# Gated cross attention and a mixture of experts: x also loaded transposed, keys centred by a second product, gamma in a second copy of the keys

## The reference, cut to what matters

```python
x = x + tanh(g_xattn[0]) * xattn(layernorm(x), ctx, W_k, b_k, gamma, beta)
x = x + tanh(g_ffn[0]) * moe(layernorm(x), ...)

def xattn(p, k_v, W_k, b_k, gamma, beta):
    kv = k_v @ W_k.T + b_k                        # keys, 256 x 64 per batch
    out = einsum('bij,bjd->bid', p, kv)           # query
    sim = einsum('bid,bjd->bij', out, kv) * 256 ** -0.5
    mu, var = mean(sim, -1), var(sim, -1)
    sim = (sim - mu) * rsqrt(var + 1e-6) * gamma + beta
    return softmax(sim, -1)
```

## Time and profile before

| | |
|---|---|
| runs, us | 206.59, 206.69, 211.18 (median 206.69) |
| span of the profiled execution | 204.2 us, 2910 instructions |
| PE busy | 186.4 us (91%) |
| DVE busy | 173.8 us (85%) |
| ACT busy | 83.5 us (41%) |
| POOL busy | 95.0 us (46%) |
| chain that ended last | PE 48%, DVE 36%, DMA 5%, issue 5%, ACT 3% |
| transfers | 18.06 MB |

### The profile page before, as it was taken

The page is one execution under the profiler, slowest core; times in us unless marked ns, Lnnn a source line. Parts: engine busy times, 40 slices in busy tenths (PEclk is TensorE's granted clock), DMA queues, the critical chain, the costliest instruction groups (busy, mean ns, idle before and its releaser), DMA issues.

```text
span 204.2 us, 2910 instructions
## 1 busy us (share of the span) xinstructions
PE 186.4 (91%) x809; PEld 142.1 (70%) x809; DVE 173.8 (85%) x332; ACT 83.5 (41%) x164; POOL 95.0 (46%) x101
## 2 busy tenths in 40 slices
PE   7899799859999979897999798999999999999992
PEld 5555578638687657575778566788888888888871
DVE  0859968999899889999889999998988989889853
ACT  2448527323349633333438314233333433434210
POOL 2252352723741746464444534446665466654500
PEclk9999979999999999999999999999999999999998
DMA  6977000003853525250211000321121122221403
GB/s 152 319 226 220 21 0 0 0 0 76 290 159 128 164 98 167 88 171 12 92 62 51 0 3 0 100 62 51 62 78 65 51 51 78 75 53 51 154 0 106
DMA packets 10264, 18.06 MB, mean 88 GB/s; under 512 B 1741, under 2 KB 3789, under 8 KB 10254
## 3 DMA queue, kind: packets, MB, share of 16 engines
q1 hardware_dynamic: 9760, 17.37, 26.7%
q10 hardware_dynamic: 494, 0.57, 1.3%
HBM read 16.82 MB, written 1.11 MB: 88 GB/s over the span
## 4 chain that ended last, share of the span: by engine, by line
PE 48%; DVE 36%; DMA 5%; issue 5%; ACT 3%; DVEq 1%; POOL 0%; SPq 0%; ACTq 0%
PE bank L794 26%; PE bank L838 14%; DVE act_hi L563 5%; DVE act_f L544 4%; DVE act_lo L566 4%; DVE weighted L536 4%; DMA xs<-x_in 3%; DVE logit L495 2%; DVE stats L458 2%; DMA w_row<-weight_rows 2%; PE bank L741 1%; PE bank L724 1%; PE bank L871 1%; DVE ln L470 1%; DVE x L514 1%
## 5 line engine op out<-in xcount | busy, mean ns | idle before, releaser
L279 POOL TENSOR_TENSOR w_lo<-w_raw,w_hi 128x256 fp32r<-128x256 f32 (+1 forms) x72 | 83.6, 1178 | 69.2 <-ACT w_hi L322 68.3
L322 ACT CAST w_hi<-w_raw 128x256 fp32r<-128x256 f32 (+2 forms) x72 | 36.7, 514 | 61.0 <-PE bank L838 36.1
L794 PE MATMUL bank<-hT_hi,w_hi 128*128 128x512 f32 x142 | 56.5, 398 | 0.0
L794 PE MATMUL bank<-hT_lo,w_hi 128*128 128x512 f32 x142 | 56.3, 396 | 0.0
L794 PE MATMUL bank<-hT_hi,w_lo 128*128 128x512 f32 x142 | 44.6, 395 | 0.0
L566 DVE TENSOR_TENSOR act_lo<-act_f,act_hi 128x512 fp32r<-128x512 f32 (+1 forms) x37 | 39.6, 1073 | 1.2
L380 ACT ACTIVATE silu_g<-bank 128x512 f32<-128x512 f32 x36 | 21.6, 600 | 31.9 <-PE bank L794 31.8
L794 PEld LDWEIGHTS bank<-hT_hi,w_lo 128*128 128x128 f32 x142 | 26.7, 188 | 6.4
L794 PEld LDWEIGHTS bank<-hT_hi,w_hi 128*128 128x128 f32 x142 | 26.7, 188 | 6.4
L838 PE MATMUL bank<-act_hi,w_hi 128*128 128x512 f32 (+1 forms) x74 | 23.6, 400 | 8.0 <-DVE act_hi L563 7.9
L794 PEld LDWEIGHTS bank<-hT_lo,w_hi 128*128 128x128 f32 x142 | 26.7, 188 | 6.1
(11 more groups left out here) (103 smaller groups left out, 143.8 us busy)
## 6 DMA issues: line engine op xcount, KB each, us to landing
w_row<-weight_rows SPq DMA_DIRECT2D x31, 256.0 KB, 3.2
w_raw<-w_in SPq DMA_DIRECT2D x18, 384.0 KB, 3.7
xs<-x_in SPq DMA_DIRECT2D x4, 256.0 KB, 5.9
out<-x SPq DMA_DIRECT2D x4, 256.0 KB, 2.8
cw<-ctxw_in ACTq DMA_DIRECT2D x1, 276.2 KB
vec<-vecs_in ACTq DMA_DIRECT2D x1, 265.0 KB, 5.6
weight_rows<-w_blk SPq DMA_DIRECT2D x4, 16.0 KB
gw<-route_in ACTq DMA_DIRECT2D x1, 16.0 KB, 6.2
```

Source lines behind the costliest of these rows:

```text
L279: nc.gpsimd.tensor_tensor(w_lo[:, par, cols], w_raw[:, bass.ds(n, 1), cols].rearrange("p o c -> p (o c)"), w_hi[:, par, cols].bitcast(F32) ...
L322: nc.scalar.copy(w_hi[:, par, cols], w_raw[:, bass.ds(n, 1), cols].rearrange("p o c -> p (o c)"))\
L794: last = nc.tensor.matmul(dst, w[:, par, w0 + c * P:w0 + (c + 1) * P], m, start=i == 0, stop=i == len(parts) - 1, skip_group_check=True)
```

## The change

x is loaded a second time, transposed on the host, and the query is formed from it as it is, without normalisation. The keys are centred: the sum of a batch's context columns, times W_k over -256, is added in the accumulator by a second product, for both layouts. The first layernorm's variance enters as an epsilon per row that is added to the similarity's variance. For batches 0 and 1 a copy of the keys times gamma gives a second similarity, and the logits are read straight from PSUM; for batches 2 and 3 DVE multiplies by gamma into `scaled`. The transposes of x, their copies, the first layer's roots and its normalisations are gone. `cw` is loaded in two parts with batch 0's context first. The orders of all engines are rewritten, and `x_stats(2)` and `x_stats(3)` stand behind `hidden_low(1)`.

```diff
-        lnT_ps = [bank[0], bank[1], bank[6], bank[7]]
-        qT_ps = [bank[2], bank[3], bank[6], bank[7]]
-        sim_ps = [bank[0], bank[1], bank[6], bank[7]]
+        kv_ps = bank[4]
+        kvT_ps = [bank[5], bank[3], bank[5], bank[3]]
+        qT_ps = [bank[2], bank[2], bank[2], bank[5]]
+        sim_ps, scaled_ps = [bank[0], bank[1], bank[6], bank[7]], [bank[6], bank[7]]
...
+            def load_x(b):
                 sp.dma_start(xs[:, 2 * b:2 * b + 2, :], x_v[:, 2 * b:2 * b + 2, :]).then_inc(x_in[b], 16)
+
+            def load_xT(b):
+                sp.dma_start(xT[:, b, :, :].rearrange("p c t -> p (c t)"), xt[b]).then_inc(xT_in[b], 16)
+
+            load_xT(0)
+            load_x(0)
+            load_xT(1)
+            load_x(1)
+            load_slice(0, 0)
+            load_xT(2)
+            load_xT(3)
+            load_slice(1, 1)
+            load_x(2)
+            load_x(3)
             ahead = 8
-            for n in range(ahead):
-                if n >= 2:
-                    sp.wait_ge(w_in[n % 2], 16 * (n // 2))
+            for n in range(2, ahead):
+                sp.wait_ge(w_in[n % 2], 16 * (n // 2))
...
-            for b in range(B):
-                root(0, b)
             pool.wait_ge(gwhi_ready, 1)
             nc.gpsimd.tensor_tensor(gw_parts[:, :, E:2 * E], gw[:], gw_parts[:, :, 0:E].bitcast(F32), ALU.subtract)\
               .then_inc(gwlo_ready, 1)
             low_gu(0, 0, 0)
             root(1, 0)
             root(1, 1)
-            pool.wait_ge(scaled_ready, 1)
-            nc.gpsimd.tensor_tensor(x1[:, 3, :], prob[:, 3, :], xs[:, 3, :], ALU.add).then_inc(x1_ready[1], 1)
             root(2, 0)
             root(2, 1)
             pool.wait_ge(hid_ready[1], 2)
...
+            first = CD + S
+            act.dma_start(cw[:, 0:first], ctxw[:, 0:first]).then_inc(ctx0_in, 16)
+            act.dma_start(cw[:, first:CD + B * S], ctxw[:, first:CD + B * S]).then_inc(ctx_in, 16)
...
             kv_copy(0)
             kvT_copy(0)
+            q_copy(0)
+            kv_copy(1)
             kvT_copy(1)
             act.wait_ge(vec_in, 16)
             nc.scalar.activation(gates[:], vec[:, V_GATES:V_GATES + 2], ACT.Tanh).then_inc(gates_ready, 1)
-            nc.scalar.activation(gamma_scaled[:], gamma, ACT.Copy, scale=SIM_SCALE).then_inc(gamma_ready, 1)
+            q_copy(1)
             act.wait_ge(gw_in, 16)
             nc.scalar.copy(gw_parts[:, :, 0:E], gw[:]).then_inc(gwhi_ready, 1)
-            ln_copy(0)
-            ln_copy(1)
-            q_copy(0)
             high_gu(0, 0, 0, 16, False)
-            kv_copy(1)
-            q_copy(1)
+            kv_copy(2)
             kvT_copy(2)
-            act.wait_ge(shift_ready, 1)
-            for t in range(HALF, NT):
-                nc.scalar.activation(ln[:, t, :], xs[:, t, :], ACT.Identity, scale=rstd[:, 0, t:t + 1],
-                                     bias=shift[:, t - HALF:t - HALF + 1]).then_inc(ln_ready[t // 2], 1)
+            kv_copy(3)
+            kvT_copy(3)
             softmax_exp(0)
-            kvT_copy(3)
-            ln_copy(2)
-            ln_copy(3)
-            softmax_exp(1)
             q_copy(2)
             q_copy(3)
-            act.wait_ge(scale_ready[1], 1)
-
-            nc.scalar.activation(prob[:, 3, :], prob[:, 3, :], ACT.Copy, scale=attn_scale[:, 3:4])\
-              .then_inc(scaled_ready, 1)
+            softmax_exp(1)
             high_d(0, 0, 0, False)
             high_gu(1, 1, 1, 16, False)
...
+            def context_sum(b):
+                nc.vector.tensor_reduce(ctx_sum[:, b:b + 1], cw[:, CD + b * S:CD + (b + 1) * S], AX.X, ALU.add)\
+                  .then_inc(ctx_sum_ready, 1)
+
+            def keys_gamma(b):
+
+                dve.wait_ge(kvT_ready, b + 1)
+                nc.vector.tensor_tensor(kvT_gamma[:, b * S:(b + 1) * S], kvT[:, b * S:(b + 1) * S],
+                                        gamma[0:CD, :], ALU.mult).then_inc(kvT_gamma_ready, 1)
 
...
             def x_stats(b):
                 dve.wait_ge(x_in[b], 16)
-                mean_var(0, b, lambda t: xs[:, t, :], 1.0, LN_EPS)
-
-            def sim_of(b, t):
-                return sim_ps[b][:, (t % 2) * S:(t % 2 + 1) * S]
+                ts = mean_var(0, b, lambda t: xs[:, t, :])
+                link(nc.vector.tensor_scalar(row_eps[:, ts], meanvar[:, 0, ts, 1], ROW_EPS, ROW_EPS * LN_EPS,
+                                             ALU.mult, ALU.add))
...
             def sim_stats(b):
                 dve.wait_ge(sim_done[b], 1)
-                mean_var(1, b, lambda t: sim_of(b, t), SIM_SCALE ** 2, SIM_EPS)
-
-            def sim_centre(b):
+                ts = mean_var(1, b, lambda t: columns(sim_ps[b], t))
+                nc.vector.tensor_tensor(var_eps[:, 1, ts], meanvar[:, 1, ts, 1], row_eps[:, ts], ALU.add)\
+                  .then_inc(var_ready, 1)
+
+            def sim_scale(b):
 
                 for t in tiles(b):
-                    nc.vector.scalar_tensor_tensor(centred[:, t, :], sim_of(b, t), meanvar[:, 1, t, 0:1], gamma_scaled[:],
-                                                   ALU.subtract, ALU.mult).then_inc(sim_read[b], 1)
+                    nc.vector.tensor_tensor(scaled[:, t - HALF, :], columns(sim_ps[b], t), gamma, ALU.mult)\
+                      .then_inc(sim_read[b], 1)
 
             def sim_logits(b, n_root):
 
+                if b < 2:
+                    dve.wait_ge(scaled_done, b + 1)
+                else:
+                    dve.wait_ge(sim_read[b], 2)
                 dve.wait_ge(rstd_ready, n_root)
-                dve.wait_ge(sim_read[b], 2)
                 for t in tiles(b):
-                    ins = nc.vector.scalar_tensor_tensor(logit[:, t, :], centred[:, t, :], rstd[:, 1, t:t + 1], beta,
+                    of = columns(scaled_ps[b], t) if b < 2 else scaled[:, t - HALF, :]
+                    ins = nc.vector.scalar_tensor_tensor(logit[:, t, :], of, rstd[:, 1, t:t + 1], beta,
                                                          ALU.mult, ALU.add)
-                link(ins)
+                    if b < 2:
+                        ins.then_inc(sim_read[b], 1)
+                if b < 2:
+                    dve.wait_ge(sim_read[b], 2)
+                else:
+                    link(ins)
                 ts = slice(2 * b, 2 * b + 2)
                 nc.vector.tensor_reduce(neg_max[:, ts], logit[:, ts, :], AX.X, ALU.max, negate=True)\
                   .then_inc(max_ready[b], 1)
...
             nc.vector.memset(zeros[:].bitcast(F32), 0.0).then_inc(zeros_ready, 1)
+            dve.wait_ge(ctx0_in, 16)
+            nc.vector.tensor_scalar(wk_mean[:], cw[:, 0:CD], -1.0 / S, None, ALU.mult).then_inc(wk_mean_ready, 1)
+            context_sum(0)
+            dve.wait_ge(ctx_in, 16)
+            context_sum(1)
             x_stats(0)
+            dve.wait_ge(vec_in, 16)
+            keys_gamma(0)
             x_stats(1)
-            normalise(0, 0, 1, xs, ln, ln_ready)
-            normalise(0, 1, 2, xs, ln, ln_ready)
-            x_stats(2)
-            x_stats(3)
-            dve.wait_ge(gamma_ready, 1)
             sim_stats(0)
-            dve.wait_ge(rstd_ready, 4)
-
-            nc.vector.scalar_tensor_tensor(shift[:], meanvar[:, 0, HALF:NT, 0], -1.0, rstd[:, 0, HALF:NT],
-                                           ALU.mult, ALU.mult).then_inc(shift_ready, 1)
-            sim_centre(0)
-            sim_logits(0, 5)
+            keys_gamma(1)
+            context_sum(2)
+            context_sum(3)
+            sim_logits(0, 1)
             sim_stats(1)
-            sim_centre(1)
-            sim_logits(1, 6)
             dve.wait_ge(gates_ready, 1)
             attention_scale(0)
             residual(0)
+            x1_stats(0)
+            sim_logits(1, 2)
+            normalise(2, 0, 3, x1, hid, hid_ready)
             attention_scale(1)
-            x1_stats(0)
-            residual(1, (2,))
+            residual(1)
             x1_stats(1)
-            normalise(2, 0, 7, x1, hid, hid_ready)
-            normalise(2, 1, 8, x1, hid, hid_ready)
             hidden_low(0)
+            normalise(2, 1, 4, x1, hid, hid_ready)
             hidden_low(1)
+            x_stats(2)
             sim_stats(2)
-            sim_centre(2)
+            sim_scale(2)
+            x_stats(3)
             dve.wait_ge(consts_ready, 2 + 2 * GROUPS - 1)
             add_logits(0)
             score_groups(0)
             each_step(dve, step, {
...
-                2: [lambda: sim_stats(3), lambda: sim_centre(3)],
-                4: [lambda: sim_logits(2, 9)],
-                5: [lambda: sim_logits(3, 10)],
+                2: [lambda: sim_stats(3), lambda: sim_scale(3)],
+                4: [lambda: sim_logits(2, 5)],
+                5: [lambda: sim_logits(3, 6)],
...
+            def project(b):
+
+                pe.wait_ge(ctx_sum_ready, b + 1)
+                if b >= 1:
+                    pe.wait_ge(kv_ready, b)
+                for t in tiles(b):
```

(61 more changed lines are left out.)

79 lines of the change are left out of this document (38 added, 41 removed).

## The result

The change made the kernel slower: 1.0268 times the time of before (95% interval 1.0221 to 1.0314), 211.47 and 212.79 us where before has 206.59 to 206.86. Some executions of the changed kernel and of several variants took 217 to 225 us, and in the three of them that were profiled (e3, e5, e6) the passes of TensorE's (PE's) head take up to twice as long; the ratios here leave out those of 221 to 225 us, and two more that lie apart (211.78 in e6, 210.67 in e12).

What follows compares the result with a forecast made beforehand. DVE's chain was taken to bound the front and first half of the experts, PE the second. Softmax at 20.35 plus 15.5 puts add_logits(0) at 35.85, 3.85 us later; 206.69 + 3.85 = 210.5 us, range 207.2 to 212.5.

Steps and rivals of the forecast that it cites:

- PE's run of 14 groups: In the head, PE's 14 groups at 0.98 us each, through ACT's key copies, hold batch 0's exponential until 18.8 us.
- rival (d): Behind add_logits(0), slack in the steps absorbs the later start and the end stays near 206.7 us; chance 0.08.
- the forecast's own case: Whole kernel as summed, add_logits(0) 3.85 us later, time 209.5 to 211.5 us; chance 0.50.
- rival (b): PE's clock falls in the new front, costing 0.5 to 1 us, or 3 on key products; 211.0 to 213.5; chance 0.15.
- the line of 2%: Whole kernel, slower by over 2%, or 4.1 us, set at 210.8 us: chance above it 0.36, within 0.58.
- The reciprocal: Batch 0's softmax on DVE, taken up at 20.35 us, 0.73 before today's 21.08.
- From there to `add_logits(0)`: DVE's stretch from batch 0's reciprocal to the start of add_logits(0), put at 15.5 us.
- The rest: From add_logits(0) to the end of the span, taken as unchanged at 172.2 us.
- The overlap of the batches: Softmaxes of batches 0 and 1 on DVE: 2.3 us given back because batch 1 follows batch 0 instead of overlapping it.
- Rival (c): In the steps, DVE regains up to 8.9 us lost to POOL, so the change is not slower; chance 0.10.
- Rival (a): PE is not the gate; POOL's root is, softmax starts at 17.6 to 19, time 207.8 to 209.2 us; chance 0.17.
- The POOL floor: In the head, POOL's root behind low_gu(0) lets batch 0's softmax start no earlier than 17.6 us; time 207.8 us.

Runs made afterwards that it cites:

- e3: Changed kernel with the softmaxes of batches 0 and 1 overlapped again on DVE and ACT; 207.40 us undisturbed, 221.37 us in the profiled execution.
- e5: Changed kernel without the second, centring product of every key group, so its output is wrong; 217.89 and 217.77 us, with PE's head as at the low clock.
- e6: The same kernel as e3, run again for a profile and more times; 207.29 to 209.19 us, ratio 1.0094 against the kernel before.
- e2: Changed kernel with batch 0's exponential ahead of the last two key copies on ACT; 209.41 and 210.37 us, ratio 1.0169 against the kernel before.
- e10: Changed kernel without the centring key products, with twelve products of zeros at the start instead of eight; 209.60 to 211.66 us, ratio 1.0229 against the kernel before.
- e7: e1 and e4 together on the changed kernel; 208.91 and 210.14 us, ratio 1.0135 against the kernel before.
- e4: Changed kernel with 14 products of zeros on PE between hidden(0) and hidden(1); 210.61 and 211.40 us, ratio 1.0223 against the kernel before.
- e11: Changed kernel with batches 0 and 1 overlapped again and twelve products of zeros at the start; 209.28 to 210.16 us, ratio 1.0132 against the kernel before.
- e9: Changed kernel with twelve products of zeros at the start in place of eight; 212.73 to 213.85 us, ratio 1.0306 against the kernel before.
- e1: Changed kernel with x_stats(2) and x_stats(3) moved into DVE's wait before attention_scale(0); 210.89 and 211.91 us, ratio 1.0242 against the kernel before.
- e8: Changed kernel with x statistics and exponentials earlier, batches overlapped, more warm products around the last queries and similarities; 209.68 to 209.86 us, ratio 1.0146 against the kernel before.
- e12: Changed kernel with its head reordered on all engines, POOL's rstd ahead of w_lo, ten products of zeros at the start; lowest times 206.39 and 207.47 us.

## Why the prediction was right, and by how much it missed

**The mechanism held.** PE's run of 14 groups is the gate of the softmax: the reciprocal follows its last copy (after), moves with what ACT copies ahead of it (e2) and with the products in it (e10). The statistics of batch 0 are 2.9 us earlier (3 to 4 was forecast), and do not matter. The later start goes through to the end: rival (d) is out, since the rest of 173.0 us is not shorter than the 172.2 of before. The time lies within the range (207.2 to 212.5) by the mean of the two executions, 212.1, and 0.3 us above it by the profiled one. It lies outside the 209.5 to 211.5 of the forecast's own case and inside rival (b)'s 211.0 to 213.5, which had 0.15. The measured loss of 2.7% lies past the line of 2%, to which the text gave 0.36 against 0.58 for "within": there the likelier case did not come.

**The miss, term by term**, for the profiled execution:

- *The reciprocal, +0.95.* PE is free at 5.04, not 4.81 (+0.23). The warm product holds it 0.43, not 0.25 (+0.18). The 14 groups take 19.59 - 5.04 - 0.43 = 14.12 us, 1.009 each where 0.98 was taken (+0.40): a project with its second products takes 1.03 to 1.04 (18.53 - 17.50, 9.74 - 8.70), so the 0.93 of the earlier trace rows was no price for it. The last products end 0.25 behind 19.59, at the low clock (0.79 instead of 0.60 us). Copy and exponential were 0.09 shorter.
- *From there to `add_logits(0)`, 15.64 against 15.5.* That the total is so close is partly luck: the last `hidden_low` ends 11.57 us behind the reciprocal (11.2 in the text, which has no low clock in this case), and what follows takes 4.07 (4.3). Two parts were tested: taking the statistics out of the open brought 2.07 (e7 against e4) where the text put 2.3, and the clock's fall on the hidden product cost 0.41 (e4) where rival (b) put 0.5 to 1. The overlap of the batches was worth 3.36 (e11 against e9) where the text put 2.3. Some 0.4 of that is the clock's: with the high clock on `hidden(1)` in both it is 2.94 (e11 against e4). The rest of the difference lies in what the text compared with: up to the end of the last `hidden_low` e4 takes 11.16, as the text has it, but e11 only 8.21, where before takes 8.9 with the low clock on its transposes.
- *The rest, +0.76*, and what lies around the span, 2.9 in place of 2.5.

**Rival (b) came on top of the forecast case, not in its place.** Its argument against itself, that PE has no gap up to 19 us, failed: in the stage from 18 to 23 us PE is busy 5.00 of 5.00 us and the clock is 0.66. The falls on steps lengthen PE's work too. One in after, in the chain of work that ended last, is a group of twelve passes that takes 2.8 to 3.0 us elsewhere in that chain:

```profile
125.71 4.12 PE bank L841 x12
```

The 0.76 us arise near these falls. DVE makes one cast `act_hi` a step; counted from `add_logits(0)` those of after start as in before at the first two, 1.18 us later at the third, near the fall from 50 to 54 us, 0.3 to 0.4 later at the ninth to the 17th, and 0.9 later from the 22nd to the last, behind the fall from 125 to 129. Whether the falls are the cause is not settled. Without falls on steps e4 has a rest of 172.0, and e1, e2, e7, e8 and e10, with some, have 173.3 to 173.7; but e9 and e11 have falls as well and 172.4 and 171.9, and e12 has none and 172.6.

**Rival (c) did not come.** Lines of DVE in after, from 39 to 133 us (busy us, mean ns), beside the earlier trace rows:

```profile
L588 DVE TENSOR_TENSOR act_lo<-act_f,act_hi 128x512 fp32r<-128x512 f32 x19 | 18.0, 946 | 0.7
L585 DVE CAST act_hi<-act_f 128x512 fp32r<-128x512 f32 x19 | 15.3, 805 | 1.8
L558 DVE TENSOR_TENSOR weighted<-silu_g,w_row 128x512 f32<-128x512 f32 x14 | 10.3, 732 | 1.4 <-ACT silu_g L390 1.3
```

The third of them in before, from 34 to 128 us:

```profile
L536 DVE TENSOR_TENSOR weighted<-silu_g,w_row 128x512 f32<-128x512 f32 x14 | 12.5, 894 | 1.4 <-ACT silu_g L380 1.3
```

The casts lose 2.3 us more than before and the subtractions 0.4, the multiplications by the weights lose 2.2 less (12.5 us before): 43.6 us together against 43.1. The sum of what is lost stayed, as the text held likely, but the overlap with POOL did not repeat as it argued: it moved from one operation to another, and nothing came back.

**Rival (a) is out**: PE is last even with half of its key products gone (e10). The POOL floor that the text gave, 17.6, would be 18.7 by the rows of after (`neg_max` ready at 17.48, exponential 1.2): `rstd` started at 15.09, 1.0 us later than in the sum behind that floor, since POOL's `w_lo` stands behind ACT's copy of the second query, and that query ended near 12.7, not at 11.6.

## What to carry to other kernels

Taking work out of the head of a chain gains nothing if another queue, here the copies on ACT behind PE's products, holds the next step; read which wait ends last before counting what is removed. Work that an engine does inside a wait is free only there: price each piece that an edit moves out of such a wait at its full duration, and test it together with the clock or the queue that would take its place, since one edit alone can show two fifths of its worth (0.81 of 2.07 us here).
